# New operation lengths in the planner that orders three engines of a fused attention and feed-forward kernel

## The chip, the cores and the metric

The kernel runs on the 8 cores of one Trainium2 chip. Each core computes one of the 8 batch entries and exchanges nothing with the others. The metric is the device time of the slowest core in microseconds (us).

## The reference, cut to what matters

```python
x = x + attn(layernorm(x), Wq, bq, Wk, bk, Wv, bv, Wo, bo)      # x: (8, 2048, 1024)
x = x + ffn(layernorm(x), W_real, W_imag, biases)
# attn: 16 heads of 64; scores / 8 + mask; softmax; @ V; @ Wo + bo
#   mask: -0.25 * log(i - j) for i > j, 0 for i == j, -inf for j > i
# ffn:  one 1024 x 1024 matrix put together from small factors G1, G2 (_unfold_tt)
```

## The kernel before

One core holds 2048 rows of x, in 16 row tiles of 128. Attention goes in 4 chunks of 512 query rows (`c`), each with 8 pairs of heads (`p`), and each pair goes through the key tiles `mt` of 128 keys up to the diagonal. Such a (c, p, mt) is a step; there are 320 (`STEPS`), 224 of them at full width, 32 each at 384, 256 and 128 query columns. A step is four operations on three engines:

- S: TensorE writes the scores of both heads (L1118, L1120, side by side on two halves of the array) to one of two score buffers `stP`. S of step g waits until the exponential of step g - 2 is done.
- X: ScalarE takes the exponential, `stP` to `PT` (L996; `PT` has 6 slots).
- P: VectorE multiplies `PT` by the power-law mask (L857).
- V: TensorE multiplies by V and by ones (L1142 into the bank `pv`, L1148 into `pr`), summed over the key tiles of the pair.

After the last V of a pair ScalarE forms the reciprocal of the denominators (Y: L1004, L1006), and VectorE scales `pv` into `attnT` (Z: L874, two instructions). There is one `pv`, so the first V of a pair waits for Z of the pair before.

Beside the steps TensorE works through groups of up to 8 passes, which share two banks `gp` in turn: T (transposes of normalised tiles), K, Q, V (projections, L1057, L1067), N and B (a bound of the scores, L1078, L1083), O (output projection, L1093) and F (feed-forward, L1103). A group may start when the bank of the group two before it has been read, an eviction E, by VectorE or ScalarE. `either` (Python function) names the groups that both engines can read: K and Q of the first three chunks and T of the first 12 tiles. VectorE also does the statistics (S1, S2), the normalisation (A), the squares (SQ) and 56 pieces of the feed-forward matrix (W, L803 and L807), which only have to be done by the middle of the attention.

Every engine works through a fixed list. `make_fill` sets which passes lie between which steps; it is the same before and after. `make_orders` takes its list as TensorE's tasks, gives each task of every engine a length in us and the tasks that it waits for, and plays the three engines forward: a free VectorE or ScalarE takes, of the tasks that are ready, the one with the earliest latest start (`late`); TensorE takes the earliest startable head of three lists (scores, values, groups), with some patience. Sixteen such plays are made (4 values of patience, 4 rounds each), and the one that ends first in the planner's own count gives `ACT_ORDER`, `DVE_ORDER` and `PE_ORDER`, as well as which engine reads which bank. The instructions then wait on semaphores, whatever the plan had thought of their time.

Of the kernel before, what the change touches and what calls it, by code (L numbers as in the profile page):

```python
# [29 lines left out]
PATIENCE = (0.1, 0.15, 0.2, 0.3)  # L30
ROUNDS = 4
# [184 lines left out]
def make_orders(plan):  # L216
# [21 lines left out]
    for k in pe:  # L238
# [8 lines left out]
        else:  # L247
# [9 lines left out]
            if k1 == PASSES[what]:  # L257
# [18 lines left out]
                us = {"B": 0.3, "T": 0.65}.get(what, 0.67)  # L276
                task("any" if either(lab) else "act" if what == "B" else "dve", ("E", lab), us, ("D", lab), *more)
    for g, (c, p, mt) in enumerate(STEPS):
        w = 1024 - 2 * trim(c, mt)
        task("act", ("X", g), 0.19 + 0.00088 * w, ("S", g), g and ("X", g - 1), g >= PR and ("V", g - PR),  # L280
             mt == 0 and p % 4 == 0 and ("BN", c, p // 4))
        task("dve", ("P", g), 0.03 + 0.00063 * w, ("X", g), ("P", g - 1) if g else ("M", 3))
    for n, g in last.items():
        task("act", ("Y", n), 0.9, ("V", g), n and ("Z", n - 1))
        task("dve", ("Z", n), 1.35, ("Y", n), n in (24, 28) and ("D", ("N", 3, 2 + (n - 24) // 4)),
             n == 16 and ("WR", 7))
    for n in range(2 * NT):
        x = [("dma", "x", n)] * 2 if n < NT else [("E", ("O", n - NT, h)) for h in range(2)]
        task("dve", ("S1", n), 0.62, x[0], n and ("S2", n - 1), n >= 4 and ("A", n - 4))
        task("dve", ("S2", n), 0.9, x[1], ("S1", n))  # L290
        task("act", ("R", n), 0.6, ("S2", n), n and ("R", n - 1))
        task("dve", ("A", n), 0.75, ("R", n), n and ("A", n - 1), n >= 2 and ("D", ("T", n - 2)))
# [6 lines left out]
    for i, (c, p) in enumerate(pairs):  # L299
        n = c * 4 + p // 2 - 2  # L300
        task("dve", ("SQ", c, p), 0.75, ("E", ("K", c, p)), ("E", ("Q", c, p)), i and ("SQ",) + pairs[i - 1],
             n >= 0 and ("D", ("N", n // 4, n % 4)))
    for c in range(NCH):
        for h in range(2):
            before = (c, 0) if h else (c - 1, 1) if c else None
            task("dve", ("BD", c, h), 0.15, ("E", ("N", c, 2 * h)), ("E", ("N", c, 2 * h + 1)), before and ("BL",) + before)
            task("act", ("BL", c, h), 0.3, ("BD", c, h), c and ("D", ("B", c - 1, h)))
            task("dve", ("BM", c, h), 0.12, ("BL", c, h), before and ("BM",) + before, c and ("D", ("B", c - 1, h)))
            task("dve", ("BN", c, h), 0.15, ("E", ("B", c, h)), before and ("BN",) + before)
# [5 lines left out]
    for i in range(56):  # L315
        task("dve", ("W", i), 0.6, ("W", i - 1) if i else ("dma", "g"), i >= 7 and i % 7 == 0 and ("WR", i // 7 - 1), i == 0 and ("M", 2))
        if i % 7 == 6:
            task("act", ("WR", i // 7), 1.4, ("W", i))
# [8 lines left out]
    def latest(pe_at):  # L327

        late = {}
        for k in tasks:  # L330
            stack = [] if k in pe_at or k in late else [k]
            while stack:
# [4 lines left out]
                else:  # L337
                    late[k] = min([pe_at.get(u, late.get(u)) for u in users[k]] + [1e4]) - tasks[k][1] - 0.12
# [3 lines left out]
    def run(late, patience):  # L342
# [11 lines left out]
        def length(k, engine):  # L354

            return tasks[k][1] + (0.4 if engine == "act" and k[0] == "E" and k[1][0] == "T" else 0.0)
# [25 lines left out]
        while any(heads.values()) or could["act"] or could["dve"]:  # L382
# [26 lines left out]
            finish(k, end + 0.12)  # L409
# [819 lines left out]
```

How the kernel before makes its waits and increments, by code:

```python
        @blk.sync  # L587
        def _(s):
            def load_x(n):
                dst, got, _ = x_tile(n)
                s.dma_start(out=dst, in_=dx[n * 128:(n + 1) * 128, :]).then_inc(got, 16)
            load_x(0)
            load_x(1)
            s.dma_start(out=ident[:, :], in_=dident).then_inc(s_ident, 16)
            load_x(2)
            load_x(3)
            s.dma_start(out=cols[:, :], in_=dcols).then_inc(s_cols, 16)
            for n in range(7, NT):
                s.wait_ge(s_xn, n - 2)
                load_x(n)
            for i in range(NT + 4):
                if i < NT:
                    if i < 3:
                        s.wait_ge(s_xn, NT - 2 + i)
                    elif i == 3:
                        s.wait_ge(s_grp, GROUP_AT[("Q", NCH - 1, PAIRS - 1)] + 1)
                    else:
                        s.wait_ge(*evicted(("O", i - 4, 1)))
                    s.dma_start(out=res_tile(i), in_=dx[i * 128:(i + 1) * 128, :]).then_inc(s_res[i % 4], 16)
                if i >= 4:
                    t = i - 4
                    for ch in range(2):
                        s.wait_ge(*evicted(("F", t, ch)))
                        o = (t % 2) * 1024 + ch * 512
                        s.dma_start(out=dout[t * 128:(t + 1) * 128, ch * 512:(ch + 1) * 512],
                                    in_=outb[:, o:o + 512]).then_inc(s_out[t % 2], 16)
            s.wait_ge(s_out[0], 16 * NT)
            s.wait_ge(s_out[1], 16 * NT)
```

## Time and profile before

| | |
|---|---|
| time, median of 3 runs | 563.18 us (561.47 to 565.92) |
| profiled execution | 561.32 us, its slowest core's span 559.8 us |
| spans of cores 0 to 7 | 557.7, 555.4, 558.1, 556.0, 557.3, 555.5, 556.2, 559.8 us |
| busy on the slowest core | TensorE 517.1 us (92%), VectorE 461.3 (82%), ScalarE 381.9 (68%) |
| instructions | 6096 matmuls, 830 on VectorE, 526 on ScalarE |
| granted TensorE clock | 0.996 of full on the slowest core, 0.999 to 1.000 on the others |

Busy time is the union of the instructions' recorded durations. A recorded duration isn't the time for which an instruction keeps its engine: where a start follows a start more closely than the recorded duration, the next one had already begun. So start to start is what the next instruction must wait, and the record is what a consumer on another engine must wait, and a little more.

### The profile page before, as it was taken

To read this page: it belongs to the slowest core of one execution; us is meant where nothing else is said; L and a number is where in the kernel's file an instruction comes from. 1 tells how busy PE (TensorE), PEld (TensorE's weight loads), DVE (VectorE), ACT (ScalarE), POOL (GpSimd) and SP (SyncE) were. 2 spreads that over 40 slices of the span, in tenths; PEclk is the share of its full clock that TensorE was granted. 3 is DMA by queue.
4 is the path that set the end of the run, shared out by engine and by line. 5 is a ranking of instruction groups with operands and counts; after the bars stand their busy time and mean duration, and the time that the engine had idled before them with its cause. 6 is when DMAs were issued, how large, how long until landed. Compare 5 with 4: busy or idle time off the path is not lost.

```text
span 559.8 us, 16753 instructions; the slowest of 8 cores (555.4 to 559.8 us)
## 1 busy us (share of the span) xinstructions
PE 517.1 (92%) x6096; PEld 241.2 (43%) x6096; DVE 461.3 (82%) x830; ACT 381.9 (68%) x526; POOL 38.3 (7%) x51
## 2 busy tenths in 40 slices
PE   1798989899999999989999999999999999999986
PEld 1334444344443444444444444444545444444442
DVE  5645999999999999887777887887888888888683
ACT  3425776778888879866767777777778777786010
POOL 7000000000000000000000020201101011111110
PEclk9999999999999999989999999999999999999999
DMA  8999231000120000010000089756566666457574
GB/s 200 187 170 253 78 114 39 3 2 2 40 78 2 8 34 1 2 47 33 1 3 2 1 121 185 150 137 148 135 152 152 152 151 141 97 130 171 146 153 150
DMA packets 16479, 52.77 MB, mean 94 GB/s; under 512 B 2000, under 2 KB 2000, under 8 KB 15632
## 3 DMA queue, kind: packets, MB, share of 16 engines
q0 software_dynamic: 7328, 28.05, 27.5%
q1 hardware_dynamic: 9072, 23.65, 12.7%
q8 instruction: 52, 0.85, 0.7%
q14 instruction: 27, 0.22, 0.1%
HBM read 51.69 MB, written 8.39 MB: 107 GB/s over the span
## 4 chain that ended last, share of the span: by engine, by line
PE 69%; DVE 9%; ACT 8%; issue 7%; DMA 5%; DVEq 0%; ACTq 0%; POOLq 0%
PE gp L1057 18%; PE stP L1118 11%; PE pv L1142 10%; PE gp L1093 8%; PE gp L1067 8%; PE gp L1103 8%; ACT PT L996 5%; PE pr L1148 4%; DMA Wo<-wo 3%; PE gp L1044 2%; DMA x<-bfn 1%; DVE stat L700 1%; DVE x L773 1%; DVE V L748 1%; DVE attnT L874 1%
## 5 line engine op out<-in xcount | busy, mean ns | idle before, releaser
L996 ACT ACTIVATE PT<-stP,negc 128x1024 bf16<-128x1024 f32 (+1 forms) x320 | 301.4, 983 | 81.8 <-PE stP L1120 80.1
L857 DVE TENSOR_TENSOR PT<-PT,decay 128x1024 bf16<-128x1024 bf16 (+1 forms) x320 | 190.7, 603 | 35.0 <-ACT PT L996 33.2
L1142 PE MATMUL pv<-PT,V 128*32 128x256 bf16 (+3 forms) x2560 | 101.4, 258 | 1.5 <-DVE PT L857 0.5
L1118 PE MATMUL stP<-QT,KT 64*128 64x512 bf16 (+1 forms) x320 | 94.5, 350 | 5.2 <-ACT PT L996 5.0
L1120 PE MATMUL stP<-QT,KT 64*128 64x512 bf16 (+1 forms) x320 | 95.1, 352 | 0.0
L1148 PE MATMUL pr<-PT,ones 128*32 128x256 bf16 (+3 forms) x1280 | 81.2, 257 | 0.7 <-issue 0.7
L1067 PE MATMUL gp<-Wv,xnT 128*128 128x512 bf16 x256 | 67.3, 385 | 8.6 <-DVE V L748 5.0
L1142 PEld LDWEIGHTS pv<-PT,V 128*32 128x32 bf16 x2560 | 56.7, 96 | 38.2 <-issue 35.9
L1057 PE MATMUL gp<-xnT,Wk 128*128 128x512 bf16 x256 | 66.7, 389 | 2.5 <-ACT xnT L968 2.0
L1057 PE MATMUL gp<-xnT,Wq 128*128 128x512 bf16 x256 | 65.0, 380 | 1.0 <-DVE KT L755 0.9
L1093 PE MATMUL gp<-Wo,attnT 128*128 128x512 bf16 x256 | 63.3, 380 | 2.4 <-DVE x L773 1.7
L1103 PE MATMUL gp<-Wf,xn2T 128*128 128x512 bf16 x256 | 63.6, 380 | 2.0 <-DVE outb L782 1.2
L1118 PEld LDWEIGHTS stP<-QT,KT 64*128 64x128 bf16 x320 | 22.6, 93 | 70.4 <-issue 67.3
L874 DVE TENSOR_TENSOR attnT<-pv,recip 64x512 bf16<-64x512 f32 x64 | 44.0, 687 | 4.8 <-ACT recip L1006 3.9
L1067 PEld LDWEIGHTS gp<-Wv,xnT 128*128 128x128 bf16 x256 | 21.6, 99 | 38.5 <-issue 20.7
L1103 PEld LDWEIGHTS gp<-Wf,xn2T 128*128 128x128 bf16 x256 | 22.8, 97 | 34.0 <-issue 11.4
L1057 PEld LDWEIGHTS gp<-xnT,Wq 128*128 128x128 bf16 x256 | 23.1, 98 | 32.3 <-issue 8.7
L1057 PEld LDWEIGHTS gp<-xnT,Wk 128*128 128x128 bf16 x256 | 22.6, 99 | 33.2 <-issue 12.6
L1093 PEld LDWEIGHTS gp<-Wo,attnT 128*128 128x128 bf16 x256 | 22.0, 97 | 34.4 <-issue 13.8
L1044 PE MATMUL gp<-ident_s,xnrot 128*128 128x128 bf16 x256 | 23.3, 233 | 14.3 <-DVE xnrot L710 13.7
L1148 PEld LDWEIGHTS pr<-PT,ones 128*32 128x32 bf16 x1280 | 34.6, 97 | 1.3 <-issue 0.8
L782 DVE TENSOR_TENSOR outb<-gp,x 128x512 f32<-128x512 f32 x32 | 22.1, 690 | 9.9 <-PE gp L1103 9.3
(71 smaller groups left out, 432.1 us busy)
## 6 DMA issues: line engine op xcount, KB each, us to landing
xrot<-x SPq DMA_DIRECT2D x21, 512.0 KB, 4.5
x<-bfn POOLq DMA_DIRECT2D x16, 512.0 KB, 6.4
out<-outb SPq DMA_DIRECT2D x32, 256.0 KB, 3.3
xrot<-bo POOLq DMA_DIRECT2D x12, 512.0 KB, 5.8
xfirst<-x SPq DMA_DIRECT2D x4, 512.0 KB, 6.2
Wk<-wk POOLq DMA_DIRECT2D x2, 1024.0 KB, 21.3
Wq<-wq POOLq DMA_DIRECT2D x2, 1024.0 KB, 27.0
Wv<-wv POOLq DMA_DIRECT2D x2, 1024.0 KB, 32.6
```

Of the source, the lines that this page charges most:

```text
L857: v.tensor_mul(pt, pt, decay[:, off + no:off + 512].unsqueeze(1).to_broadcast([128, 2, 512 - no])).then_inc(s_pm, 1)
L874: ins = v.tensor_mul(out, pv[x:x + 64, :].rearrange("p (d m q) -> p d m q", d=2, q=64), recip[x:x + 64, :].rearrange("p (m q) -> p m q", q ...
L996: a.activation(p_tile(g, no), st_tile(g, no), AF.Exp, bias=negc[:, c * 8 + p % 2 * 4 + p // 2:][:, 0:1]).then_inc(s_exp, 1)
L1044: ins = t.transpose(ps[:, :].bitcast(BF16)[:, k * 128:(k + 1) * 128], xnrot[:, o + k * 128:o + (k + 1) * 128], ident[:, 0:128])
L1057: ins = t.matmul(ps[:, :], W[:, o:o + 128], xnTv[:, k, :], start=(k == 0), stop=(k == FT - 1))
L1067: ins = t.matmul(ps[:, :], xnTv[:, k, j * 128:(j + 1) * 128], Wv[:, half * 4096 + k * 512:half * 4096 + (k + 1) * 512], start=(k == 0), st ...
L1093: ins = t.matmul(ps[:, :], attnT[:, o + k * 512:o + k * 512 + 128], Wo[:, k * D + ch * 512:k * D + (ch + 1) * 512], start=(k == 0), stop=( ...
L1103: ins = t.matmul(ps[:, :], xn2Tv[:, i % 2, k], Wf[:, k * D + ch * 512:k * D + (ch + 1) * 512], start=(k == 0), stop=(k == FT - 1))
L1118: t.matmul(stP[g % 2][:, no:512], KT[0:64, ks:ks + 128], QT[0:64, qs + no:qs + 512], start=True, stop=True, tile_position=(0, 0))
L1120: t.matmul(stP[g % 2][:, 512 + no:1024], KT[64:128, ks:ks + 128], QT[64:128, qs + no:qs + 512], start=True, stop=True, tile_position=(64, ...
L1142: t.matmul(pv[x:x + 32, half * 256 + no // 2:(half + 1) * 256], V[:, vo + h * 64 + half * 32:vo + h * 64 + half * 32 + 32], p_part(g, h, a ...
L1148: ins = t.matmul(pr[x:x + 32, no // 2:256], ones32[:, :], p_part(g, h, a, no), start=first, stop=last, tile_position=(0, x), skip_group_ch ...
```

## The change

The lengths in `make_orders` are replaced, and with them the time between an operation's end on ScalarE or VectorE and its readiness for the others, now `LAG`. Nothing else is changed, and no operation is added or removed.

```diff
+LAG = 0.18
...
-                us = {"B": 0.3, "T": 0.65}.get(what, 0.67)
+                us = {"B": 0.25, "K": 0.67, "Q": 0.67}.get(what, 0.61)
...
-        task("act", ("X", g), 0.19 + 0.00088 * w, ("S", g), g and ("X", g - 1), g >= PR and ("V", g - PR),
+        task("act", ("X", g), 0.14 + 0.000853 * w, ("S", g), g and ("X", g - 1), g >= PR and ("V", g - PR),
...
-        task("dve", ("P", g), 0.03 + 0.00063 * w, ("X", g), ("P", g - 1) if g else ("M", 3))
+        task("dve", ("P", g), 0.068 + 0.00052 * w, ("X", g), ("P", g - 1) if g else ("M", 3))
     for n, g in last.items():
-        task("act", ("Y", n), 0.9, ("V", g), n and ("Z", n - 1))
-        task("dve", ("Z", n), 1.35, ("Y", n), n in (24, 28) and ("D", ("N", 3, 2 + (n - 24) // 4)),
+        task("act", ("Y", n), 0.8, ("V", g), n and ("Z", n - 1))
+        task("dve", ("Z", n), 1.22, ("Y", n), n in (24, 28) and ("D", ("N", 3, 2 + (n - 24) // 4)),
...
-        task("dve", ("S2", n), 0.9, x[1], ("S1", n))
-        task("act", ("R", n), 0.6, ("S2", n), n and ("R", n - 1))
-        task("dve", ("A", n), 0.75, ("R", n), n and ("A", n - 1), n >= 2 and ("D", ("T", n - 2)))
+        task("dve", ("S2", n), 0.83, x[1], ("S1", n))
+        task("act", ("R", n), 0.53, ("S2", n), n and ("R", n - 1))
+        task("dve", ("A", n), 0.72, ("R", n), n and ("A", n - 1), n >= 2 and ("D", ("T", n - 2)))
...
-        task("dve", ("SQ", c, p), 0.75, ("E", ("K", c, p)), ("E", ("Q", c, p)), i and ("SQ",) + pairs[i - 1],
+        task("dve", ("SQ", c, p), 0.67, ("E", ("K", c, p)), ("E", ("Q", c, p)), i and ("SQ",) + pairs[i - 1],
...
-            task("act", ("WR", i // 7), 1.4, ("W", i))
+            task("act", ("WR", i // 7), 1.05, ("W", i))
...
-                    late[k] = min([pe_at.get(u, late.get(u)) for u in users[k]] + [1e4]) - tasks[k][1] - 0.12
+                    late[k] = min([pe_at.get(u, late.get(u)) for u in users[k]] + [1e4]) - tasks[k][1] - LAG
...
-            return tasks[k][1] + (0.4 if engine == "act" and k[0] == "E" and k[1][0] == "T" else 0.0)
+            more = {"T": 0.31, "K": -0.08, "Q": -0.08}.get(k[1][0], 0.0) if engine == "act" and k[0] == "E" else 0.0
+            return tasks[k][1] + more
...
-            finish(k, end + 0.12)
+            finish(k, end + LAG)
```

What the lists then hold: the first 101 entries of TensorE's list and its last 241, the first 22 and last 20 of ScalarE's and the first 36 and last 25 of VectorE's are what they were. Of TensorE's 2248 entries 1965 keep their place in the list. In between, single steps and passes change places with their neighbours. TensorE changes between scores, values and groups at 541 places before and 522 now. ScalarE reads 48 banks, before 50: K of pairs 5, 6 and 7 of the first chunk go to VectorE, tile 9's T goes to ScalarE, and in the second and third chunk six Q come to ScalarE and K 2,0, 2,1, 2,3 and 2,6 with Q 1,4 and 2,4 leave it. The W pieces stand earlier: the last behind mask product 107 before and behind 100 now.

TensorE between the last V of pair 2 of the second chunk (the 32x64 rows) and the next pair's steps; `ident_s,xnrot` is T of tile 9, `Wv,xnT` V of tile 6, `lsel` B. Before:

```order
309 L1142 MATMUL pv<-PT,V 32x64 x8
310 L1148 MATMUL pr<-PT,ones_58 32x64 x4
311 L1044 MATMUL gp<-ident_s,xnrot 128x128 x8
312 L1118 MATMUL stP<-QT,KT 128x512
313 L1120 MATMUL stP<-QT,KT 128x512
314 L1067 MATMUL gp<-Wv,xnT 128x512 x2
315 L1083 MATMUL gp<-lsel,cols_s 128x8
316 L1118 MATMUL stP<-QT,KT 128x512
317 L1120 MATMUL stP<-QT,KT 128x512
318 L1067 MATMUL gp<-Wv,xnT 128x512 x6
```

And now:

```order
308 L1144 MATMUL pv<-PT,V 32x64 x8
309 L1150 MATMUL pr<-PT,ones_58 32x64 x4
310 L1046 MATMUL gp<-ident_s,xnrot 128x128 x8
311 L1120 MATMUL stP<-QT,KT 128x512
312 L1122 MATMUL stP<-QT,KT 128x512
313 L1069 MATMUL gp<-Wv,xnT 128x512 x2
314 L1144 MATMUL pv<-PT,V 32x256 x8
315 L1150 MATMUL pr<-PT,ones_58 32x256 x4
316 L1085 MATMUL gp<-lsel,cols_s 128x8
317 L1120 MATMUL stP<-QT,KT 128x512
```

Before, the next pair's first V stood at row 324; now it stands behind two passes of V of tile 6, ahead of B. The changed program's line numbers are larger by 2.

VectorE at the same place; L874 (L876) is Z of the pair. Before:

```order
220 L828 TENSOR_REDUCE nrmx<-nrm 128x2
221 L736 COPY xnT<-gp 128x8x128
222 L857 TENSOR_TENSOR PT<-PT,decay 128x1024
223 L839 TENSOR_TENSOR lsel<-cols_s,nrmx 128x8
224 L874 TENSOR_TENSOR attnT<-pv,recip 64x8x64 x2
```

And now:

```order
227 L830 TENSOR_REDUCE nrmx<-nrm 128x2
228 L859 TENSOR_TENSOR PT<-PT,decay 128x1024
229 L712 TENSOR_SCALAR xnrot<-xrot,stat 128x1024
230 L876 TENSOR_TENSOR attnT<-pv,recip 64x8x64 x2
231 L841 TENSOR_TENSOR lsel<-cols_s,nrmx 128x8
```

The copy of tile 9's bank has gone to ScalarE, a normalisation has come ahead of Z, and `lsel`, for which B waits, stands behind Z.

TensorE in the first chunk, where the first V of pair 2 and V of tile 1 (second half) meet; before, these rows began with the eight passes and the 32x256 rows came behind the transposes and the next scores. Now:

```order
62 L1120 MATMUL stP<-QT,KT 128x128
63 L1122 MATMUL stP<-QT,KT 128x128
64 L1144 MATMUL pv<-PT,V 32x256 x8
65 L1150 MATMUL pr<-PT,ones_58 32x256 x4
66 L1069 MATMUL gp<-Wv,xnT 128x512 x8
67 L1046 MATMUL gp<-ident_s,xnrot 128x128 x8
```

The first V of the pair has moved ahead of a whole group. On VectorE's list Z of pair 1 now stands ahead of the reading of V tile 0 (second half), before behind it.

## Rows read from the trace of the kernel before

**Rows 1.** Windows: us, busy time of PE, PEld, DVE, ACT, POOL, clock, DMA share, GB/s.

```profile
36.00:60.00 24.00, 21.83 (x151) 9.83 (x153) 13.86 (x30) 10.74 (x18) 0.00 (x0) 1.00 0.88 216
60.00:340.00 280.00, 265.97 (x3354) 122.34 (x3351) 250.81 (x469) 217.23 (x308) 3.58 (x4) 0.99 0.13 31
340.00:514.00 174.00, 170.76 (x2206) 80.69 (x2206) 147.46 (x253) 134.61 (x167) 19.82 (x24) 1.00 0.62 144
```

**Rows 2.** Waits of PE over the span: us in total, times, longest.

```profile
PE gp L1044 <- DVE xnrot L710: 13.7, 4, 8.8
PE gp L1067 <- DVE V L748: 5.0, 10, 1.2
PE stP L1118 <- ACT PT L996: 5.0, 18, 0.6
```

**Rows 3.** Groups of full-width X and P, and of Z: busy, mean ns, idle before.

```profile
L996 ACT ACTIVATE PT<-stP,negc 128x1024 bf16<-128x1024 f32 x224 | 241.5, 1111 | 63.6 <-PE stP L1120 62.1 <-DVE negc L847 1.0 <-issue 0.3
L857 DVE TENSOR_TENSOR PT<-PT,decay 128x1024 bf16<-128x1024 bf16 x224 | 151.7, 683 | 25.9 <-ACT PT L996 24.8
L874 DVE TENSOR_TENSOR attnT<-pv,recip 64x512 bf16<-64x512 f32 x64 | 44.0, 687 | 4.8 <-ACT recip L1006 3.9
```

**Rows 4.** Timeline of DVE: start, duration, instruction.

```profile
185.47 1.39 DVE L874 TENSOR_TENSOR attnT<-pv,recip 64x512 bf16<-64x512 f32 x2
186.89 0.69 DVE L857 TENSOR_TENSOR PT<-PT,decay 128x1024 bf16<-128x1024 bf16 x1
187.50 0.69 DVE L807 TENSOR_TENSOR wacc<-wacc,wtmp 128x512 f32<-128x512 f32 x1
```

**Rows 5.** Timeline of ACT, back to back.

```profile
185.08 1.11 ACT L996 ACTIVATE PT<-stP,negc 128x1024 bf16<-128x1024 f32 x1
186.10 0.68 ACT L943 ACTIVATE KT<-gp,cols_s 128x512 bf16<-128x512 f32 x1
```

**Rows 6.** Timeline of PE: values after values, scores after values.

```profile
189.13 0.39 PE L1142 MATMUL pv<-PT,V 128*32 128x256 bf16 x8
...
189.45 0.39 PE L1142 MATMUL pv<-PT,V 128*32 128x256 bf16 x8
...
190.21 0.40 PE L1142 MATMUL pv<-PT,V 128*32 128x256 bf16 x8
...
190.65 0.28 PE L1118 MATMUL stP<-QT,KT 64*128 64x256 bf16 x1
```

**Rows 7.** Timeline, pair border with little delay: last V, Y, Z, first V.

```profile
99.78 0.20 PE L1148 MATMUL pr<-PT,ones 128*32 128x64 bf16 x4
...
100.19 0.38 ACT L1004 ACTIVATE recip<-pr 128x256 f32<-128x256 f32 x1
...
101.48 1.39 DVE L874 TENSOR_TENSOR attnT<-pv,recip 64x512 bf16<-64x512 f32 x2
...
103.02 0.40 PE L1142 MATMUL pv<-PT,V 128*32 128x256 bf16 x8
```

**Rows 8.** Timeline of PE at the first place of the change.

```profile
147.96 0.20 PE L1148 MATMUL pr<-PT,ones 128*32 128x64 bf16 x4
...
149.76 0.59 PE L1067 MATMUL gp<-Wv,xnT 128*128 128x512 bf16 x2 [0.73 <-DVE xnT L736]
150.33 0.36 PE L1083 MATMUL gp<-lsel,cols_s 128*128 128x8 f32 x2
150.62 0.39 PE L1118 MATMUL stP<-QT,KT 64*128 64x512 bf16 x1
```

**Rows 9.** Timeline there: ACT's second half of Y, DVE's copy and Z.

```profile
148.84 0.42 ACT L1006 ACTIVATE recip<-recip 128x256 f32<-128x256 f32 x1
```

**Rows 10.** DVE there.

```profile
148.82 0.69 DVE L736 COPY xnT<-gp 128x1024 bf16<-128x1024 bf16 x1 [0.21 <-PE gp L1044]
...
150.10 1.38 DVE L874 TENSOR_TENSOR attnT<-pv,recip 64x512 bf16<-64x512 f32 x2
```

**Rows 11.** PE at the second place.

```profile
68.16 1.89 PE L1067 MATMUL gp<-Wv,xnT 128*128 128x512 bf16 x8 [0.70 <-DVE V L748]
```

More of the change, by code:

```diff
@@ L288, in make_orders @@
         x = [("dma", "x", n)] * 2 if n < NT else [("E", ("O", n - NT, h)) for h in range(2)]
-        task("dve", ("S1", n), 0.62, x[0], n and ("S2", n - 1), n >= 4 and ("A", n - 4))
-        task("dve", ("S2", n), 0.9, x[1], ("S1", n))
-        task("act", ("R", n), 0.6, ("S2", n), n and ("R", n - 1))
-        task("dve", ("A", n), 0.75, ("R", n), n and ("A", n - 1), n >= 2 and ("D", ("T", n - 2)))
+        task("dve", ("S1", n), 0.6, x[0], n and ("S2", n - 1), n >= 4 and ("A", n - 4))
+        task("dve", ("S2", n), 0.83, x[1], ("S1", n))
+        task("act", ("R", n), 0.53, ("S2", n), n and ("R", n - 1))
+        task("dve", ("A", n), 0.72, ("R", n), n and ("A", n - 1), n >= 2 and ("D", ("T", n - 2)))
         if n < NT:
@@ L305, in make_orders @@
             before = (c, 0) if h else (c - 1, 1) if c else None
[L306 to L309, printed above, removed]
+            task("dve", ("BD", c, h), 0.13, ("E", ("N", c, 2 * h)), ("E", ("N", c, 2 * h + 1)), before and ("BL",) + before)
+            task("act", ("BL", c, h), 0.19, ("BD", c, h), c and ("D", ("B", c - 1, h)))
+            task("dve", ("BM", c, h), 0.08, ("BL", c, h), before and ("BM",) + before, c and ("D", ("B", c - 1, h)))
+            task("dve", ("BN", c, h), 0.08, ("E", ("B", c, h)), before and ("BN",) + before)
     task("dve", ("M", 0), 2.8, ("A", 3))
```

## The prediction

> **What bounds the kernel now.** I began with the busy time of the engines by stretch [rows 1], because the change moves nothing ahead of 36 us and nothing behind about 514 us. TensorE is busy 21.83 of 24 us, 265.97 of 280 and 170.76 of 174: it sets the end, and all its idle time in these stretches is 2.2 + 14.0 + 3.2 = 19.4 us. VectorE is at 250.81 of 280, but part of that is W pieces that only fill its gaps. So the change has two ways to gain: less idle time of TensorE, or less work of TensorE. It has 19.4 us for the first.
>
> The waits say what the idle time is [rows 2]. The largest, 13.7 us for normalised tiles, lies in the start and stays. The rest is small: 10 waits of together 5.0 us for a reading of a V bank by VectorE, 18 of 5.0 us for an exponential. The longest of these is 1.2 us. There is no single hole to close, only some dozens of short ones.
>
> Then the lengths, since they are the whole change. A recorded X of 1024 columns is 1111 ns, a P 683, one of the two instructions of Z 687 [rows 3]. On VectorE a W starts 0.61 us behind a P [rows 4], though P's record is 0.69: the engine is free about 0.08 us before the record ends. On ScalarE a K reading starts 1.02 us behind X [rows 5], 0.09 before X's record ends. The old lengths (P: 0.03 + 0.00063 x 1024 = 0.675; X: 0.19 + 0.00088 x 1024 = 1.09; a reading: 0.67) are near the records, the new ones (0.600, 1.013, 0.61) near the distance from start to start. For these the new plan is the truer one.
>
> Not so for Z. Its two instructions run from 185.47, and the next one starts at 186.89, 1.42 us later [rows 4]. Here nothing overlaps. The old length was 1.35, the new one is 1.22: it was 0.07 short and is now 0.20 short. And Z is on a path: the first V of the next pair waits for it.
>
> **What the change is worth, part by part.** The time from X's start to P's start was planned as 1.09 + 0.12 = 1.21 us and is now 1.013 + 0.18 = 1.19; for P 0.795 and 0.78; for a bank reading 0.79 and 0.79. So how far TensorE's work must stand from its source hardly moves. Only the room on VectorE and ScalarE grows, by about 0.075 us an operation. This is why 1965 of 2248 entries keep their place, and why I expect small numbers.
>
> *Fewer changes of kind on TensorE.* Values start 0.32 us behind values, but scores 0.44 behind values [rows 6]: a change costs 0.12 here. It went from 541 to 522 changes. 19 x 0.12 = 2.3 us at most; others, where the pass before is long, hide a part, and I take 0.10 each: **-1.9 us**, with 0 and -2.3 as ends. It is TensorE's own work and nothing hides it.
>
> *The first place, after pair 2 of the second chunk.* The chain at such a border [rows 7]: the last `pr` ends at 99.98, Y starts 0.21 later, Z starts 1.29 behind Y, takes 1.39, and the first V starts 0.15 behind it. From the end of `pr` to the first V are 3.04 us; some 0.3 of this was Z queued on VectorE. So 2.7 us is the least. In the change the next first V stands behind T, a step's scores and two passes: 8 x 0.055 + 0.22 + 2 x 0.22 + four changes of 0.10 = 1.5 us. TensorE must wait up to 2.7 - 1.5 = 1.2 us. Part of that was paid before at the same point, since the two passes start only at 149.76 after a wait of 0.73 for VectorE's copy of tile 9 [rows 8], which ran from 148.82 [rows 10]. This copy now goes to ScalarE, behind Y, whose second half starts at 148.84 [rows 9], so it starts near 149.16, takes 1.0 (0.31 more than on VectorE), and the passes start near 150.4. Z starts no later than before: the copy left VectorE (0.61) and the normalisation (0.72) came ahead of Z, so at about 150.1 [rows 10] or a little sooner, and V can start at 1.53 behind it, near 151.5. B and the next scores, which started at 150.33 and 150.62 [rows 8], stand behind it, near 151.9 and 152.1. The scores lose 1.5 us and V's own 0.43 us is done earlier: **+1.1 us**. Ends: 0, where ScalarE and VectorE had room that I don't see, and +1.5.
>
> *The second place, first chunk, pair 2.* The first V of the pair now stands ahead of eight passes that start at 68.16 behind the reading of the V bank [rows 11]. VectorE has taken Z ahead of that reading. Z takes 1.39 where the reading takes 0.69, so the passes start about 1.0 us later (1.42 + 0.61 against 0.70 + the 0.3 by which Z can start sooner), less the 0.43 of V already done: **+0.5 us**, between 0 and +1.0.
>
> *Other places.* The same exchange in the other direction: after pair 5 of the first chunk (the border of [rows 7]) the first V has moved back behind five passes, and room grows from 2.4 us to 3.9. Such gains I take at **-0.3 us**; the ends are -2 and +2 us, which is a fifth of the 10 us in the second and third line of [rows 2], since most orders around those waits are the same as before.
>
> *Readers of the banks.* Three K readings of the first chunk go from ScalarE to VectorE, where each takes some 0.67 us from start to start. They fall in 46 to 64 us, and VectorE is busy 13.86 of 24 us up to 60 us [rows 1]: 2.0 us fit into its 10 us of room. Cost nothing; if a P were queued behind them, one K reading's 0.67 us. In the second and third chunk both engines give up and get as much. W pieces standing 7 products earlier take no longer; each can hold an urgent reading for 0.61 us, as before. Nothing.
>
> *DMA.* No transfer is moved, and the load of Wo is still released by the last K group, with the same list behind it up to the first output projection.
>
> Sum: -1.9 + 1.1 + 0.5 - 0.3 = **-0.6 us**. On the profiled execution that is 561.3 - 0.6 = 560.7. The median of the runs shown is 563.2, 1.9 above it, and the answer is wanted against such runs: **562.6 us**.
>
> **A rule that speaks against the new lengths.** The rows show that VectorE starts an operation 0.08 us before the record of the one ahead ends [rows 4]. The Trainium skill ("VectorE: DVE Perf Modes", section on the DRAIN you can't avoid) says that the next operation doesn't start until the pipe has emptied. By that rule the old 0.675 would be right and the new 0.600 too short, and the change would hurt; it is rival 4. The trace disagrees for P and W and agrees only for Z.
>
> **Rivals.**
>
> 1. *The truer lengths dissolve the waits.* If the new plan avoids four tenths of the 19.4 us of idle time [rows 1], 7.8 us, beside the 1.9 us: 563.2 - 9.7 = 553.5. For it: fourteen us of the idle time lie in the stretch where VectorE is near full and where the planner's room was most wrong. Against: the longest waits stand at places whose order did not change, and no delay between engines moved by more than 0.02 us. From three tenths (-5.8 and -1.9) it counts as clearly faster. 0.17.
>
> 2. *Z's length turns the plan over.* There are 31 pair borders. If at each the first V is planned 0.19 to 0.20 us too early (1.42 - 1.22), where before it was 0.07, and the steps queued behind it on TensorE carry the delay on, that is 31 x 0.20 = 6.2 us; with the first two places' 1.6 and less the 1.9: 563.2 + 5.9 = 569.1. For it: [rows 4], and the first two places. Against: only four borders have less than the 2.7 us of work between (three before), the others have 3.5 to 9 us, and there Z is hidden. It decides where the list leaves under 2.7 us at more than about six borders. 0.10.
>
> 3. *The change does nothing that can be seen.* The moved entries are neighbours, engines wait at the same places, the 19 changes lay beside waits: 563.2. Within the same band as the forecast. 0.15.
>
> 4. *VectorE isn't free before its record ends.* Then each reading by VectorE in the new plan is 0.08 short; over about 130 readings 10.4 us less 1.9: 571.7. The starts in [rows 4] speak against it directly. 0.02.
>
> **How the numbers follow.** The forecast has 0.56. Its own range is 562.6 - 3.5 to 562.6 + 4: the ends of the terms (-2.3, 0, 0, -2 give -4.3; 0, 1.5, 1.0, 2 give +4.5) rarely fall together. Two runs of one kernel differ by up to 4.5 us (561.47 to 565.92), which a median of three reduces; what can be told from no change is about 1%, 5.6 us. The range for 8 in 10 takes in part of rivals 1 and 2, which are cut at half their size: 557.0 to 568.0. Faster by over 1% is rival 1 with a little of the forecast's lower end (0.18). Slower by over 1% is rivals 2 and 4 with almost nothing of the forecast (0.12). The rest, 0.70, is within 1%.
>
> **What would show it right or wrong.** The windows from 60 to 514 us would show TensorE's busy time lower by about 2 us, since its records count the gaps between kinds that the pipeline covers, and idle time within 2 us of 17.2. In the timeline near 150 us TensorE should stand for about 1 us in front of a `pv` row with VectorE's `attnT` as its releaser; before, no such wait is among the large ones [rows 2]. Near 68 us the group behind the first V should start near 69. The waits for V banks and for exponentials should stay between 3 and 7 us each. If the idle time of TensorE between 60 and 514 us falls below 12 us, the sum is wrong in its fourth term and rival 1 holds; if waits for `attnT` add up to more than 4 us, rival 2 does. The start up to 36 us and the end from the last 241 entries on should be as long as before, within what the arrival of x and of the weights moves.

## The result, and the profile after

The changed kernel takes 573.01 us, median of 4 runs (571.67 to 575.24). The kernel before took 564.55 us (561.47 to 566.12, 4 runs) beside it. The ratio is 1.0161, 95% interval 1.0125 to 1.0196: slower by 1.6%, where I had forecast no change and a range that ended at 568.0. The time given with each run below is the median of all its executions, while every ratio leaves out those in which the cores of a die ran at a lower clock throughout; where the two disagree, the ratio counts.

The profiled execution took 573.36 us. The spans of cores 0 to 7 are 563.3, 569.1, 570.3, 565.8, 564.0, 567.2, 566.7 and 571.7 us: every core is longer (before 555.4 to 559.8), and they lie 8.4 us apart instead of 4.4. Windows of the slowest core, columns as in [rows 1]:

```profile
36.00:60.00 24.00, 21.05 (x150) 9.22 (x149) 13.66 (x29) 9.36 (x16) 0.00 (x0) 1.00 0.97 222
60.00:340.00 280.00, 260.95 (x3292) 120.08 (x3291) 249.60 (x467) 214.02 (x304) 3.58 (x4) 0.99 0.11 28
340.00:514.00 174.00, 166.34 (x2135) 78.80 (x2133) 140.65 (x242) 129.37 (x162) 18.65 (x22) 0.98 0.64 140
```

Against [rows 1] TensorE stands idle 2.95 + 19.05 + 7.66 = 29.7 us, before 19.4. The waits, as in [rows 2]:

```profile
PE gp L1046 <- DVE xnrot L712: 14.1, 4, 9.2
PE stP L1120 <- ACT PT L998: 5.3, 12, 1.1
PE gp L1069 <- DVE V L750: 5.1, 9, 1.2
PE gp L1095 <- DMA Wo<-wo: 4.3, 1, 4.3
PE pv L1144 <- DVE attnT L876: 2.2, 3, 1.0
PE gp L1059 <- DVE KT L757: 2.1, 3, 0.9
```

The first three kinds are within 0.4 us of before. Grown are the wait for the load of Wo (0.3 us on this core before), those for Z (0.5 before) and those for K readings by VectorE (0.9 before). No row holds the whole loss. The recorded lengths did not move (X and P of full width, Z; [rows 3]):

```profile
L998 ACT ACTIVATE PT<-stP,negc 128x1024 bf16<-128x1024 f32 x224 | 240.8, 1110 | 70.0 <-PE stP L1122 67.2 <-PE pr L1150 1.7 <-DVE negc L849 0.5
L859 DVE TENSOR_TENSOR PT<-PT,decay 128x1024 bf16<-128x1024 bf16 x224 | 152.0, 685 | 38.3 <-ACT PT L998 37.3
L876 DVE TENSOR_TENSOR attnT<-pv,recip 64x512 bf16<-64x512 f32 x64 | 44.0, 687 | 4.3 <-ACT recip L1008 3.2
```

**Where the time is lost.** I followed the same work through both traces: the start of X of steps 2, 56, 96, 190, 205 and 319, the mean of the 8 cores. Differences to the kernel before in each of the five stretches between them are +4.4, +0.9, +1.1, +1.2 and +2.3 us. Nearly half of the loss has happened by step 56, which starts at 146.8 us on core 3 before and at 152.3 now. The same stretch of core 3 shows how. Before (one row for 60 to 100 us, one for 100 to 146):

```profile
60.00:100.00 40.00, 37.17 (x433) 17.60 (x432) 38.73 (x80) 29.88 (x57) 0.00 (x0) 1.00 0.23 68
100.00:146.00 46.00, 43.45 (x527) 19.59 (x525) 44.77 (x85) 35.57 (x54) 0.00 (x0) 1.00 0.02 3
```

And after:

```profile
60.00:100.00 40.00, 35.75 (x381) 16.66 (x380) 38.75 (x78) 27.77 (x54) 0.00 (x0) 1.00 0.24 68
100.00:146.00 46.00, 41.84 (x517) 18.81 (x514) 44.71 (x85) 34.69 (x53) 0.00 (x0) 1.00 0.01 2
```

VectorE is busy 38.7 of 40 us and then 44.7 of 46 in both: here it is fuller than TensorE and has next to nothing spare. What differs is TensorE, 37.17 against 35.75 us and 43.45 against 41.84. VectorE did the same amount of work, but from 100 to 146 us 20 W pieces were in it where 17 were before, work that nobody waited for yet. From 60 to 100 us there are 5 in both, so there the W pieces don't tell the two kernels apart; the second place, looked at below, lies in that stretch.

**The half clock.** The granted clock falls to its lower level (1.2 GHz) for 3.4 us at a time in some places. Worked out from each core's mean clock, as stretches of 3.4 us, that happened 0.46 times a core before (52 runs) and 1.87 times after. In the profiled execution all 8 cores have such a stretch at 156 to 159 us, just behind the first place of the change; cores 1, 2 and 7 another at 348 us (on core 7 twice as long), and core 5 two more at 84 and 108 us. Core 0, behind the first place:

```profile
154.83 0.59 PE L1069 MATMUL gp<-Wv,xnT 128*128 128x512 bf16 x2 [1.47 <-ACT xnT L970]
155.70 0.40 PE L1144 MATMUL pv<-PT,V 128*32 128x256 bf16 x8 [0.28 <-DVE attnT L876]
156.14 0.39 PE L1085 MATMUL gp<-lsel,cols_s 128*128 128x8 f32 x2
156.79 2.74 PE L1069 MATMUL gp<-Wv,xnT 128*128 128x512 bf16 x6
```

The last row is six passes in 2.74 us; two take 0.59 in the first row. My estimate from the length is that a stretch of 3.4 us at half speed costs up to 1.7 us.

### The profile page after: what moved, and what is told of

It reads as the page before. It is cut to its first block, busy times and chain, and to the rows that moved or that the text cites. A ratio compares the mean times of both kernels' runs of the same rounds, so it can differ in the third digit from the quotient of the medians.

```text
span 571.7 us, 16753 instructions; the slowest of 8 cores (563.3 to 571.7 us)
## 1 busy us (share of the span) xinstructions
PE 519.0 (91%) x6096; PEld 241.9 (42%) x6096; DVE 462.7 (81%) x832; ACT 381.2 (67%) x524; POOL 38.3 (7%) x51
## 4 chain that ended last, share of the span: by engine, by line
PE 63%; DVE 13%; issue 9%; ACT 7%; DMA 7%; SPq 0%; DVEq 0%; ACTq 0%; POOLq 0%
PE gp L1059 16%; PE stP L1120 10%; PE pv L1144 9%; PE gp L1095 8%; PE gp L1069 7%; PE gp L1105 7%; ACT PT L998 5%; DMA Wo<-wo 4%; PE pr L1150 4%; DMA cols_s<-cols 3%; DVE attnT L876 2%; DVE PT L859 2%; DVE x L775 1%; PE gp L1046 1%; DVE V L750 1%
## 5 line engine op out<-in xcount | busy, mean ns | idle before, releaser
L1095 PE MATMUL gp<-Wo,attnT 128*128 128x512 bf16 x256 | 64.5, 386 | 7.5 <-DMA Wo<-wo 4.3
L876 DVE TENSOR_TENSOR attnT<-pv,recip 64x512 bf16<-64x512 f32 x64 | 44.0, 687 | 4.3 <-ACT recip L1008 3.2
L1095 PEld LDWEIGHTS gp<-Wo,attnT 128*128 128x128 bf16 x256 | 22.3, 98 | 40.5 <-issue 20.4
L1046 PE MATMUL gp<-ident_s,xnrot 128*128 128x128 bf16 x256 | 23.0, 230 | 16.3 <-DVE xnrot L712 14.1
```

Source lines behind the costliest of these rows:

```text
L876: ins = v.tensor_mul(out, pv[x:x + 64, :].rearrange("p (d m q) -> p d m q", d=2, q=64), recip[x:x + 64, :].rearrange("p (m q) -> p m q", q ...
L1046: ins = t.transpose(ps[:, :].bitcast(BF16)[:, k * 128:(k + 1) * 128], xnrot[:, o + k * 128:o + (k + 1) * 128], ident[:, 0:128])
L1095: ins = t.matmul(ps[:, :], attnT[:, o + k * 512:o + k * 512 + 128], Wo[:, k * D + ch * 512:k * D + (ch + 1) * 512], start=(k == 0), stop=( ...
```

## The experiments

In what follows "step 2 to 56" and so on are the means of the 8 cores less the kernel before, with half of each half-clock stretch taken out, so that waits alone remain. They come from one profiled execution a kernel. For the changed kernel the five stretches are then +4.0, -0.8, +1.3, +0.4 and +2.3 us. Each expectation names its own theories.

### The two named places, the clock and Wo

**e1_place1.** The orders around the first place put back.

```diff
+move(PE_ORDER, ("V", 56), ("S", 61))
+ACT_ORDER.remove(("E", ("T", 9)))
+DVE_ORDER.insert(DVE_ORDER.index(("BD", 1, 1)) + 1, ("E", ("T", 9)))
+move(DVE_ORDER, ("BM", 1, 1), ("P", 56))
+move(DVE_ORDER, ("Z", 10), ("BM", 1, 1))
+move(DVE_ORDER, ("P", 57), ("Z", 10))
+move(DVE_ORDER, ("A", 11), ("P", 57))
```

> The changed kernel with its orders at the first place (after pair 2 of the second chunk) put back as before: the next first V behind the later scores, tile 9's bank read by VectorE, B's selection ahead of Z. Theory A (few places, each a wait with a half-clock stretch behind it): in the trace of the change this place costs 3.3 us between about 150 and 160 us, 1.6 of waiting and 1.7 for 3.4 us at half clock on all cores. Without it the half-clock stretch near 157 us goes on every core and the time falls by 2 to 4 us, to about 570. Theory B (Z too short in the plan, many borders each late by a little): one place of 31 changes the time by under 1 us.

Measured: 572.6 us (568.77 to 575.21, 4 runs), ratio 1.0148 (1.0087 to 1.0209). The scores of step 61 start 3.0 us sooner than in the changed kernel (mean of the cores), and those of step 62 already 0.5 us later: what the place gave was lost again at once. Core 3 (behind Z at L890; a W piece, the first half of a tile's statistics, their second half and sum, the V reading; then TensorE's group):

```profile
154.51 1.38 DVE L890 TENSOR_TENSOR attnT<-pv,recip 64x512 bf16<-64x512 f32 x2
...
157.26 0.69 DVE L823 TENSOR_TENSOR wacc<-wacc,wtmp 128x512 f32<-128x512 f32 x1
157.86 0.69 DVE L709 BATCH_NORM_STATS2 stat<-xrot 128x6 f32<-128x512 f32 x1
...
159.12 0.69 DVE L716 BATCH_NORM_STATS2 stat<-xrot 128x6 f32<-128x512 f32 x1
159.91 0.21 DVE L718 BATCH_NORM_AGGREGATE stat<-stat 128x2 f32<-128x12 f32 x1
160.16 0.69 DVE L764 TENSOR_TENSOR V<-gp,bvB 128x512 bf16<-128x512 f32 x1
...
161.10 1.46 PE L1083 MATMUL gp<-Wv,xnT 128*128 128x512 bf16 x6 [2.58 <-DVE V L764]
```

The kernel before, core 3, in the same place:

```profile
149.77 1.38 DVE L874 TENSOR_TENSOR attnT<-pv,recip 64x512 bf16<-64x512 f32 x2
151.18 0.69 DVE L857 TENSOR_TENSOR PT<-PT,decay 128x1024 bf16<-128x1024 bf16 x1
151.79 0.81 DVE L710 TENSOR_SCALAR xnrot<-xrot,stat 128x1024 bf16<-128x1024 f32 x1
152.63 0.69 DVE L748 TENSOR_TENSOR V<-gp,bvB 128x512 bf16<-128x512 f32 x1
```

The reading that TensorE's group waits for starts 1.5 us behind the end of Z before and 4.3 us here. A W piece and a tile's statistics, which stood behind it, now stand ahead of it, and VectorE worked them off without a gap. The edit did not put these back. So the orders that the prediction named aren't what the changed kernel loses by; a hole closed on TensorE opens at the next reading that VectorE has behind work that could wait.

**e2_place2.** The second place put back: V of step 8 behind the next scores, Z 1 behind the V reading.

```diff
+move(PE_ORDER, ("V", 8), ("S", 13))
+move(DVE_ORDER, ("Z", 1), ("E", ("V", 0, 1)))
```

> The changed kernel with its orders at the second place (first chunk, pair 2) put back: first V behind the scores of step 13, the reading of the V bank ahead of Z. The trace shows PE 1.0 us before V for Z and 0.3 for the bank, and 1.2 to 1.4 us lost at this place on every core. Theory A: the spans fall by about 1.2 us. Theory B: under 0.5 us. The median may not show it against runs that differ by some us.

Measured: 573.24 us (5 runs), ratio 1.0158 (1.0097 to 1.0218). Step 2 to 56 is +2.9 instead of +4.0: the place is worth 1.1 us. The total kept none of it; half-clock stretches rose from 1.9 to 2.6 a core.

**e3_fill.** Six useless passes of 512 columns into a free bank, ahead of the group at the first place.

```diff
+for _ in range(6):
+    t.matmul(bank(("B", 1, 1))[:, :], KT[:, 0:128], KT[:, 0:512], start=True, stop=True)
```

> The changed kernel with six useless matmuls of 512 columns into the free bank gp in front of the wait of 1.5 us at the first place; orders and waits stay, the output too. If the half clock behind this place comes from TensorE standing still there, the granted clock near 157 us stays at 2.4 GHz and the time falls by 1.7 us against the change, to about 571, though the wait itself is as long. If the half clock has another source, the clock stretch stays and the time is that of the change or up to 0.3 us more.

Measured: 572.89 us (4 runs), ratio 1.0157 (1.0095 to 1.022). The half-clock stretch at 157 us is gone on all 8 cores. Core 0 in the same place:

```profile
153.41 1.47 PE L1157 MATMUL gp<-KT 128*128 128x512 bf16 x6
154.87 0.59 PE L1069 MATMUL gp<-Wv,xnT 128*128 128x512 bf16 x2
155.83 0.40 PE L1144 MATMUL pv<-PT,V 128*32 128x256 bf16 x8 [0.37 <-DVE attnT L876]
156.27 0.39 PE L1085 MATMUL gp<-lsel,cols_s 128*128 128x8 f32 x2
156.59 0.39 PE L1120 MATMUL stP<-QT,KT 64*128 64x512 bf16 x1
156.59 0.39 PE L1122 MATMUL stP<-QT,KT 64*128 64x512 bf16 x1
156.91 1.47 PE L1069 MATMUL gp<-Wv,xnT 128*128 128x512 bf16 x6
```

The same six passes take 1.47 instead of 2.74 us. With the first of the two waits in front filled, the drop here is gone. But there are stretches near 83, 250 and 350 us on cores that had none there, and the slowest core gained nothing. The cores without one took 562.8 us, still 5 more than before: the clock is not the whole loss.

**e4_wo_halves.** Wo loaded in two halves, the first released four K groups earlier.

```diff
-            g.wait_ge(s_grp, GROUP_AT[("K", NCH - 1, PAIRS - 1)] + 1)
+            for half, p in enumerate((3, 7)):
+                g.wait_ge(s_grp, GROUP_AT[("K", NCH - 1, p)] + 1)
```

> The changed kernel with Wo loaded in two halves, the first released by the K group of pair 3 of the last chunk, the second by that of pair 7. In the trace of the change three cores wait up to 4.3 us for Wo near 346 us and run 3.4 to 6.8 us at half clock behind it; their spans are 569 to 572 us, those of the others 563 to 567. Theory A (the loss on the slowest core is mostly here): no wait for Wo on any core, no half clock near 350 us, slowest core 566 to 568, time falls by 4 to 6 us. Theory B (Z, many borders): the time falls by under 1.5 us.

Measured: 569.06 us (7 runs), ratio 1.0089 (1.005 to 1.0128): 4 us better than the changed kernel. The edit does two things, it splits the load and starts its first half sooner, and the two aren't told apart. Wo from issue to landing (KB each, median us) on the slowest core of the changed kernel:

```profile
Wo<-wo POOLq DMA_DIRECT2D x1, 2048.0 KB, 22.3
```

And in halves:

```profile
Wo<-wo POOLq DMA_DIRECT2D x2, 1024.0 KB, 10.3
```

Before, it was 17.8 us on the slowest core and 16.3 to 18.6 on all. In the changed kernel cores 1, 2 and 7, its three slowest, took 21.4 to 22.3 us and the others 16.5 to 18.1. The halves took 9.1 to 12.4 us (the median of a core's two). With the halves no core drops its clock near 350 us, and the spans lie 4.0 us apart instead of 7.8. Wo makes the slow cores slower; of the loss in the mean of the cores it makes a quarter (564.8 us, changed 566.8, before 558.5).

### Which work fills VectorE

**f1_w_late.** The 56 W pieces and their roundings put back behind the products where they stood before.

```diff
+DVE_ORDER = [k for k in DVE_ORDER if k[0] != "W"]
+    DVE_ORDER.insert(DVE_ORDER.index(("P", W_BEHIND[_n])) + 1, ("W", _n))
```

> The changed kernel with only the 56 W pieces (and ScalarE's 8 roundings of them) put back behind the mask products behind which they stand before; nothing else moves. Theory C (VectorE is the bound from about 70 to 200 us; the new plan, believing its operations shorter than they are, gives it four more W pieces by mask product 55 and three more bank readings, together 4 x 0.6 + 3 x 0.67 = 4.4 us of work, and TensorE comes as much later): the four W pieces are 2.4 us, so the cores without half-clock stretches fall from about 563 to about 560.5 us, and the loss against before at step 54 from 4.3 to about 2 us. Theory A (the first two pair borders and the clock): no change at step 54 but for 0.5 us, and the same half-clock stretches. The median should fall by 2 to 4 us by C, by under 1 by A.

Measured: ratio 1.035 (1.0301 to 1.0399), which is some 585 us; the median of the four executions is 598.01 (584.2 to 647.51). A miss, and a lesson on the method: pieces put behind a product land ahead of whatever urgent reading stands there now. The slowest core has

```profile
PE stP L1128 <- ACT PT L1006: 9.0, 12, 2.4
...
PE gp L1067 <- DVE nrm L778: 3.3, 2, 3.1
```

It doesn't test the number of pieces.

**f2_k_act.** K readings of pairs 5, 6 and 7 of the first chunk back on ScalarE.

```diff
+for _p, _behind in ((5, ("R", 4)), (6, ("Y", 0)), (7, ("R", 5))):
+    DVE_ORDER.remove(("E", ("K", 0, _p)))
```

> The changed kernel with only the readings of the K banks of pairs 5, 6 and 7 of the first chunk given back to ScalarE, where they stood. Theory C: 3 x 0.67 = 2.0 us less on VectorE ahead of the stretch in which it is the bound, so up to 2 us less on each core; less, down to 0, where VectorE still had room at 50 to 65 us (it is busy 13.7 of 24 us up to 60 us). Theory A: nothing, within 0.3 us.

Measured: 571.9 us (4 runs), ratio 1.0102 (1.0041 to 1.0162). Step 2 to 56 is +3.5 instead of +4.0: of 2.0 us taken from VectorE 0.5 came back. The interval overlaps that of the changed kernel.

**f3_w_late_k_act.** Both.

> Both together: W pieces as late as before and the three K readings on ScalarE; the new orders of everything else stay, the two pair borders with their waits too. Theory C: the loss at step 54 falls from 4.3 to under 1.5 us; cores without half-clock stretches come to 558 to 560 us, the time to 565 to 568. Theory A: at most 1 us below the change's 573.

Measured: 583.48 us (4 runs), ratio 1.03 (1.025 to 1.0349). It has the fault of f1 and missed both theories.

**f4_dve_old.** No order moved by hand: the planner of the change with VectorE's lengths as before; ScalarE's lengths and `LAG` are the new ones.

```diff
-        task("dve", ("P", g), 0.068 + 0.00052 * w, ...
+        task("dve", ("P", g), 0.03 + 0.00063 * w, ...
-        task("dve", ("Z", n), 1.22, ...
+        task("dve", ("Z", n), 1.35, ...
```

(and readings 0.67, S1 0.62, S2 0.9, A 0.75, SQ 0.75, and the three small operations of the bound of the scores; the change had shortened S1 and these too, by 0.02 to 0.07 us)

> The changed kernel's planner with VectorE's lengths as before (mask products, bank readings, statistics, squares, scaling), ScalarE's lengths and the new lag kept; planned anew. At mask product 55 its list holds 22 W pieces and 30 bank readings, as against 22 and 32 before and 26 and 35 in the change. Theory C: VectorE has no more to do by then than before, so no loss at step 54 (within 1 us), cores near 557 us, time near before's 563.5. Theory B (Z's length and what goes with it): Z's old 1.35 is in here too, so it also says better than the change. If the loss stays, it lies in ScalarE's lengths or the lag.

Measured: 561.22 us (558.21 to 565.05, 6 runs), ratio 0.9947 (0.9895 to 0.9999). Step 2 to 56 is -0.6. So VectorE's lengths carry the whole loss, and the rest of the change gains a little, by an interval that ends just short of 1. This tempers the reading of the windows above: on core 3 from 60 to 100 us TensorE is busy only 36.54 us in this run, less than before, and yet the run is as fast. A single window does not decide; the times of the steps do.

**h1_load.** The kernel before with seven useless VectorE operations of 0.6 us between products 19 and 54.

```diff
+LOAD_BEHIND = (19, 25, 31, 37, 43, 49, 54)
...
+                    if n[0] in LOAD_BEHIND:
+                        v.reduce_max(spare[:, :], decay[:, 0:512], AX.X)
```

> The kernel before, its orders untouched, with seven useless reductions of 512 columns of about 0.6 us on VectorE, behind mask products 19, 25, 31, 37, 43, 49 and 54 (about 90 to 147 us). Theory C (VectorE is the bound there, so work added to it comes out one for one): TensorE is 4.2 us later at step 56, the cores without half-clock stretches go from 556.5 to about 560.7, and the time from 564 to about 568.5, more where the longer waits bring half-clock stretches. If TensorE is the bound there and the waits come from single places in the order, most of the 4.2 us is hidden: under 1.5 us.

Measured: 567.54 us (10 runs), ratio 1.0062 (1.0025 to 1.0099). Of 4.2 us put on VectorE 3.0 appear in step 2 to 56, 2.2 of them with the half clock taken out. In the whole time it is about 3.5 us by the ratio. Most of what is added to VectorE in this stretch is paid, in orders that are otherwise those of before.

### Which of the lengths

**h3_b_lag.** The kernel before, the delay alone from 0.12 to 0.18.

> The kernel before with only the lag between an operation's end and its readers raised from 0.12 to 0.18, all lengths as before. Planned anew: 20 W pieces and 33 bank readings by mask product 55, that is 0.6 us less VectorE work than before, but 582 changes of kind on TensorE instead of 541. Theory C: no loss at step 54 (within 1 us). The 41 more changes cost about 4 us by 0.10 each if nothing hides them; so the time is 563 to 568, and the lag is not what made the change slow.

Measured: 561.5 us (10 runs), ratio 0.9948 (0.991 to 0.9987). Better than the expectation had it, and with 582 changes of kind on TensorE, where before has 541. It is also as good as f4_dve_old, so the delay may be all that the rest of the change gains.

**h2_a_z141.** The changed kernel, Z alone from 1.22 to 1.41.

> The changed kernel's planner with one length corrected: Z at 1.41 us, as start to start in the trace, instead of 1.22. Planned anew: 23 W pieces and 35 bank readings by mask product 55 (change 26 and 35, before 22 and 32), and a pair border of 1.8 us instead of 1.5 at the first place. Theory B (Z is the mis-sized length that matters): no loss at step 54, time at before's 564. Theory C: 0.6 + 2.0 = 2.6 us more VectorE work than before by then, so a loss of about 2.6 us at step 54 and a time of 567 to 570.

Measured: 566.49 us (10 runs), ratio 1.0052 (1.002 to 1.0084). One number takes back 6.5 us (6.1 by the ratios). Step 2 to 56 is +0.3 instead of +4.0, and 23 W pieces stand ahead of product 55 instead of 26 (before 22). The 35 bank readings there are those of the changed kernel (before 32), so theory C, which priced the added work at 2.6 us, missed: three readings and one W piece more than before cost 0.3 us once the plan's Z is long enough. Theory B is right to step 56, but the ratio stays above 1; +1.4 us are lost in the stretch from step 96 to 190.

**m1_b_z122.** The other way round: the kernel before, Z alone from 1.35 to 1.22.

> The kernel before with one number changed: Z 1.35 to 1.22. Theory A (Z's length is the cause by itself): the loss of Z's correction in the changed kernel, 6.5 us, comes back here: 569 to 572, and step 2 to 56 is 2 us or more longer. Theory B (Z's length hurts only together with short products and readings, since only then VectorE is planned fuller than it can be; W pieces ahead of mask product 55 are 21 here, 22 before, 26 changed): 561 to 566, step 2 to 56 within 1 us of before.

Measured: 568.71 us (12 runs), ratio 1.0063 (1.0028 to 1.0098). Between the theories: step 2 to 56 is only +0.6, as B said, but half-clock stretches rose to 1.37 a core and the slowest core is 3.9 us longer; cores without one took 558.0 us, before 557.4.

**m2_a_pe_old.** The changed kernel, products and readings at their old lengths, Z short.

> The changed kernel with the lengths of mask products and bank readings as before, Z short at 1.22 as changed. W pieces ahead of mask product 55: 24 (changed 26, before 22). Theory A (Z by itself): 569 to 573. Theory B (both needed): 562 to 567. Theory C (the products' and readings' lengths do nothing, Z with the other new lengths does): as A, but with more than 1.2 half-clock stretches a core.

Measured: 564.4 us (12 runs), ratio 0.9995 (0.9954 to 1.0037). Theory B. Step 2 to 56 is +1.2.

**m3_exact.** The changed kernel with Z, S2 and the delay from TensorE to its reader as the trace shows them.

```diff
-        task("dve", ("Z", n), 1.22, ...
+        task("dve", ("Z", n), 1.54, ...
-        task("dve", ("S2", n), 0.83, x[1], ("S1", n))
+        task("dve", ("S2", n), 0.97, x[1], ("S1", n))
-                finish(k, free["pe"] + 0.17)
+                finish(k, free["pe"] + 0.33)
```

> The changed kernel with Z 1.54 (what the trace shows from the end of Y to the first V's start, less the delay), S2 0.97, and 0.33 us instead of 0.17 from a TensorE task to its reader. Products and readings stay short, at start to start. 552 changes of kind on TensorE. Theory A (each length must be right, and short products and readings do no harm once Z and the delay are right): 558 to 562, step 2 to 56 within 1 us of before. Theory B (the padding of 0.07 us an operation in the old lengths was useful room by itself): 564 to 568, step 2 to 56 at +2 or more.

Measured: 560.95 us (559.62 to 564.56, 12 runs), ratio 0.9956 (0.9917 to 0.9996). Theory A: short products and readings do no harm once Z, S2 and the delay are right. Core 3 in 60 to 100 us:

```profile
60.00:100.00 40.00, 37.26 (x433) 17.32 (x431) 38.50 (x81) 30.32 (x58) 0.00 (x0) 1.00 0.26 85
```

TensorE is back at 37.26 with VectorE at 38.50. Z, S2 and the delay from TensorE moved together here, so what each gives beyond h2_a_z141 (566.49) isn't told apart. With Z alone right, at 1.41, the ratio was still 1.0052.

**h4_best.** f4_dve_old and the two halves of Wo together.

> The best version that these results point to: VectorE's lengths as before, ScalarE's lengths and the lag of the change, and Wo loaded in two halves. The orders alone gave 561.2 beside before's 565.4 in one set of runs; half a load of Wo earlier takes away the waits for it of up to 5 us on single cores and the half clock behind them, worth 1 to 3 us on the slowest core. 557 to 561 us, 0.5 to 1.2% under before. If the load of Wo was late on no core of that version, 561.

Measured: 559.33 us (11 runs), ratio 0.9915 (0.9885 to 0.9946), the best version; it beats the kernel before by 0.85%. What the halves add to f4_dve_old is smaller than the intervals. Spans lie 4.1 us apart, half-clock stretches are 0.39 a core.

## Why the prediction was wrong

**What is shown.** The four corners:

| | P and readings short | at their old lengths |
|---|---|---|
| Z 1.22 | 1.0161 (changed kernel) | 0.9995 |
| Z 1.35 or 1.41 | 1.0052 | 0.9947 |

The corner at the lower right, f4_dve_old, has VectorE's other lengths old as well, so it is not a clean one. Z counts for 1.1% with short readings, which is clear of noise, and for 0.5% with old ones, which is not; the cleaner pair, the kernel before and m1_b_z122, gives 0.6% (0.3 to 1.0). That the two errors are worse together than one by one is what the stretch to step 56 says: Z takes 3.7 us off with short readings, 1.8 with old ones, and makes 0.6 in the kernel before. The times alone don't show it: the difference between 1.1 and 0.5% is smaller than its error.

What follows is the account that fits these runs; that Z's length carries most of the loss is shown, the way from it to the wait is in part argued. The old lengths had padding, 0.075 us for each product, and Z's error of 0.07 us disappeared in it. The change took the padding away, rightly by the rows, and made Z's error 0.20. Then the plan promises VectorE more than it can do, and from 60 to 146 us VectorE has nothing spare to catch up with. Work that isn't urgent, ahead of its time in the plan's belief, is done ahead of work that is: the W piece and the statistics ahead of the V reading in e1_place1. The amount of work doesn't explain it by itself. Ahead of product 55 the changed kernel has 4.4 us more VectorE work than before (4 W pieces of 0.6 us, 3 readings of 0.67) and loses 4.0; m2_a_pe_old has 2.5 us more (2 and 2) and loses 1.2; h2_a_z141 has 2.6 more (1 and 3) and loses 0.3. The second place shows what a Z that takes longer than planned does to its neighbours, core 7 after:

```profile
68.19 0.42 ACT L1008 ACTIVATE recip<-recip 128x256 f32<-128x256 f32 x1
...
67.91 0.67 DVE L770 TENSOR_REDUCE nrm<-gp 128x1 f32<-128x512 f32 x1
68.49 0.68 DVE L859 TENSOR_TENSOR PT<-PT,decay 128x1024 bf16<-128x1024 bf16 x1
69.20 1.39 DVE L876 TENSOR_TENSOR attnT<-pv,recip 64x512 bf16<-64x512 f32 x2
70.62 0.69 DVE L750 TENSOR_TENSOR V<-gp,bvB 128x512 bf16<-128x512 f32 x1
...
70.74 0.40 PE L1144 MATMUL pv<-PT,V 128*32 128x256 bf16 x8 [1.03 <-DVE attnT L876]
71.57 1.89 PE L1069 MATMUL gp<-Wv,xnT 128*128 128x512 bf16 x8 [0.32 <-DVE V L750]
```

Z's input is there at 68.61, Z starts at 69.20, and the next operation only 1.42 us later: the plan believed 1.22. TensorE stands 1.03 us, and 0.32 more for the reading behind Z.

**Point by point.**

- *The failed step: the sum puts at nothing what the lengths do to VectorE's list.* "Only the room on VectorE and ScalarE grows", three K readings "cost nothing", the W pieces "nothing", and Z's error is counted only where a first V waits for it. Up to step 56 the sum had one loss, the second place with +0.5; measured are +4.0 us. Z's number alone takes back 3.7 of them (h2), VectorE's old lengths all (f4). Of the +4.0 the second place is 1.1 (e2) and the K readings 0.5 (f2); how the rest divides between W pieces and the order of the other work, no run shows.
- *Why it looked like nothing.* I judged VectorE's room by 36 to 60 us, 13.86 of 24 us busy. I had 250.81 of 280 for the next stretch [rows 1] and did not cut it finer: 38.7 of 40 us from 60 to 100 and 44.8 of 46 after that. Most of what enters there is paid: h1_load pays 3.0 of 4.2 us.
- *"No delay between engines moved by more than 0.02 us".* Wrong for the one that mattered. Z with its delay was planned as 1.35 + 0.12 = 1.47 us and is now 1.22 + 0.18 = 1.40, where [rows 7] have 1.39 + 0.15 = 1.54. A K or Q reading by VectorE went the other way, from 0.79 to 0.85.
- *The lengths, "for these the new plan is the truer one", "not so for Z".* Right, both, and m3_exact fits. But I priced Z's error only where a first V waits for Z (rival 2: borders with little work). Waits for Z grew from 0.5 to 2.2 us a core and Z's number alone took back 6.5 us (h2), so most of its price came by other ways: other readings that came late, half-clock stretches (1.87 a core, 0.86 with the right Z) and the wait for Wo (4.3 us on the slowest core, at most 1.0 on any with the right Z).
- *Idle time from 60 to 514 us within 2 us of 17.2, waits for V banks and exponentials 3 to 7 us each.* The waits are 5.1 and 5.3, but the idle time is 26.7: the rows that I had named held still while the loss went in under other names.
- *Rival 2, 569.1 at 0.10.* The right cause by the wrong path. Its own sign, waits for `attnT` over 4 us, did not come: they are 2.2 us.
- *The first place, +1.1.* Half right. The passes came at 154.83 behind the copy on ScalarE, as forecast, but the long wait was for that copy, 1.47 us on core 0, and V waited for Z only 0.28 us and not about 1. The half clock behind it, up to 1.7 us, was not in the sum. Together they move the scores of step 61 by 3.0 us, and putting the orders back (e1) changed the time by nothing that can be told.
- *The second place, +0.5.* Mechanism right, size 1.1 (e2), a little over its upper end.
- *Fewer changes of kind, -1.9.* Not seen. The fastest edit of a single length (h3) has 41 more changes than before and is faster; whatever the changes cost, it is outweighed.
- *"No transfer is moved."* True, and yet Wo landed in 21 to 22 us on three cores and cost the slowest one 4.3 us. What the list does not move can still arrive at a worse time.
- *Rival 4, that VectorE is not free before its record ends.* Refuted again: W pieces follow a product after 0.61 us in the trace after, and m3_exact, planned with these distances, is as good as f4_dve_old with padding. The Trainium skill ("VectorE: DVE Perf Modes", section on the DRAIN you can't avoid) says that the next operation waits for the empty pipe, but adds that one which is not held starts earlier; I had left the second half out. The trace has both: 0.61 us behind records of 0.69, and 1.42 us behind Z's records of 1.39.

**What stays open.** Why Wo lands later on those three cores was not settled. f1 and f3 leave the price of W pieces alone untested, and no run put only the order of bank readings and statistics back. Why a half-clock stretch comes on one core and not on its neighbour with the same orders, I can't say; in e2 and e3 it moved to other places when one was closed. m1 loses more than its waits explain, by these stretches.

## What to carry to other kernels

A planner's lengths must be right relative to each other: where most of them carry some padding, it can hide the error of one that is too short, and taking the padding away from the others was worse here than leaving it (1.0161 against 0.9995 with Z short). Before costing work on a helper engine at nothing, cut its busy share into windows of 20 to 40 us and look at the fullest one; there most of the helper's time is the kernel's time (3.0 of 4.2 us here). Ask also in what order a full helper will do its work, not only how much it has. And on many cores read the spread as well as the mean: a transfer that lands late on three of eight cores can be half of the loss in the time of the slowest (4 of 8.5 us here).

## What was not expected of the hardware

- Waits that add up to 1.75 us (1.47 and 0.28, core 0) were followed by 3.4 us at the 1.2 GHz level on all 8 cores; with the first of them filled by useless passes (0.37 us left) on none.
- The same 2048 KB load took 16.5 to 18.1 us from issue to landing on five cores and 21.4 to 22.3 on three, in one execution; as halves of 1024 KB 9.1 to 12.4 us.
- VectorE overlaps 0.08 us of one operation's record with the next for products and readings, and nothing behind either of Z's two instructions, whose operands take 64 partitions; no run here tests whether the partitions are the reason.
